# Which engine makes the low half of each expert weight: 24 on GpSimd, none on VectorE

## The chip, the cores and the metric

One core of a Trainium2 chip runs the whole program. The metric is the device time of one execution in microseconds (us), lower is better; a kernel's time is the median of its runs. In this text PE is TensorE, DVE is VectorE, ACT is ScalarE, POOL is GpSimd and SP is SyncE, which here only issues DMAs.

## The reference

Four batches of 1,024 tokens with 256 channels pass a cross attention to 64 context rows and then a mixture-of-experts feed-forward layer, each on a layer-normalised input and added to its residual.

```python
x = x + _L0_xattn_ref(_layernorm(x), ctx_768, Wq, bq, Wk, bk, Wv, bv, Wo, bo)   # 16 heads
# _L0_ffn_ref on the layer-normalised x, T = 4096 tokens, D = 256, H = 512, E = 8 experts, top 2
shared = _swiglu(xf, sh_gate, sh_up, sh_down)
w, idx = jax.lax.top_k(jax.nn.softmax(xf @ gate_w.T), 2)
comb = zeros((T, E)).at[arange(T)[:, None], idx].add(w / w.sum(-1))
g = silu(einsum('td,ehd->teh', xf, eg)); u = einsum('td,ehd->teh', xf, eu)
out = shared + einsum('ted,te->td', einsum('teh,edh->ted', g * u, ed), comb)
```

(The argument names are shortened.) All data are float32.

## The kernel before

TensorE multiplies in float16. To keep float32's accuracy each operand is held as two float16 numbers, a high half (the value rounded) and a low half (the value less its high half), and each product is the sum of three: high by high, high by low, low by high.

**The weights.** There are 27 weight matrices of 128 x 1024 numbers, numbered q: 0 to 2 are the shared expert's gate, up and down, and 3 to 26 are those of the 8 experts. Matrix q goes through four steps. SP loads it in float32 into slot q % 4 of a ring of four, `w_stage` (`load_w`, L449), and for q >= 4 first waits until q - 4 is split. ACT rounds it into its high half (`split_hi`, L705). Then one engine subtracts to make the low half: POOL (L629) where q is odd, DVE (`split_lo`, L960) where q is even. That subtraction counts up the semaphore `w_lo[q % 4]`, for which SP waits, and PE before it starts the experts (`weights_split`).

**Three stages.** Up to about 310 us runs the attention. Then comes the *shared stage*: 32 steps k, each a chunk of 128 hidden units of the shared expert on a group of 512 tokens (four steps make a group). Last comes the *expert stage*, 46 slots of gathered tokens.

**A step k of the shared stage.** PE does `up(k)` (24 matmuls of 512 columns, gate and up; the trace lists them in twelves) and then `down(k-1)` (12 matmuls of 256 columns). ACT runs SiLU (L764), in some steps a part of the second layer norm (`norm2`, L750 and L757), then `split_hi`, then the high half of the hidden activations (L778). DVE multiplies gate and up (L1150), at each group's first step adds the group before to `x_sb` (`add_shared`, L1190), in some steps does the layer norm's low half (`low_half`, L989, for which the transposes on SP's queue wait, L471) and reads the router's logits (L995); then comes `split_lo`, and last the low half of the hidden activations (L1183), for which `down(k)` on PE waits. Everything on an engine runs in program order.

**Which matrix in which step.** A table, `SPLITS`, gives the steps k = 2 to 13 the matrices q = k + 1 (3 to 14), and the steps k = 19 to 30 the matrices q = k - 4 (15 to 26). POOL follows by `w_hi`, the count of high halves. The routing runs on DVE in between: `best_two` at k = 11 (L1017 to L1036, ahead of matrix 12's split), `weights` and `places_in_expert` at k = 13 (L1041 to L1089, ahead of matrix 14's), and one-hot maps up to k = 18.

**POOL's queue** around the end of the shared stage: after matrix 21 (k = 25) it issues the stores of five finished groups of output (L622), a store of spare rows (L633) and the gathers for the first three expert slots (L603, four indirect DMAs); only then come its remaining splits, then the last three output stores, and the gathers and scatters of the expert stage.

The lines of `split_lo` and of POOL's loop:

```python
for q in range(1, 3 * (E + 1), 2):                      # POOL
    pool.wait_ge(w_hi, q + 1)
    pool.tensor_tensor(w[:, 1], w_stage[:, q % 4, :], w[:, 0], ALU.subtract).then_inc(w_lo[q % 4], 1)
    if q == 21:
        ...
if q % 2 == 0:                                          # DVE, split_lo(q)
    dve.wait_ge(w_hi, q + 1)
    dve.tensor_tensor(w[:, 1], w_stage[:, q % 4, :], w[:, 0], ALU.subtract).then_inc(w_lo[q % 4], 1)
```

Of the kernel before, what the change touches and what calls it, by code (L numbers as in the profile page):

```python
# [17 lines left out]
def build(nc, x, ctx_t, wq, bq, wk, bk, wv, bv, wo, bo, gate_t, w_all, out):  # L18
# [3 lines left out]
    E = w_all.shape[0] // 3 - 1  # L22
# [39 lines left out]
    with ExitStack() as ctx:  # L62
        def sb(name, shape, dt):
            return ctx.enter_context(nc.sbuf_tensor(name, shape, dt))
# [9 lines left out]
        w_sh = sb("w_sh", [P, 3, 2, 1024], F16)  # L74
        arena = sb("arena", [P, E * 3 * 2 * 1024], F16)
        w_rt = arena[:, :].rearrange("p (e m s n) -> p e m s n", e=E, m=3, s=2)
        w_qs = arena[:, :].rearrange("p (q s n) -> p q s n", q=3 * E, s=2)
# [429 lines left out]
        def _(pool):  # L507
# [90 lines left out]
            def gather(n):  # L598
                for r, i in zip(buffers(n), columns(n)):
                    if rank_of[n] >= 2:  # L600
                        pool.wait_ge(xt_got[r], 16 * uses(n))
                        pool.wait_ge(sp_w, same_kind(n, 2) + 1)
                    pool.indirect_dma_start(  # L603
                        out=gathered(r), out_offset=None, in_=rows_d,
                        in_offset=bass.IndirectOffsetOnAxis(ap=map_i[:, 0, i:i + 1], axis=0)).then_inc(x_got[r], 16)
# [14 lines left out]
            def store_out(g):  # L620
                pool.wait_ge(ffn_added, g + 1)
                pool.dma_start(out_tiles[:, g * GT:(g + 1) * GT, :],  # L622
                               x_sb[:, g * GT:(g + 1) * GT, :]).then_inc(out_stored, 16)

            AHEAD = 3
            for q in range(1, 3 * (E + 1), 2):
                w = w_sh[:, q] if q < 3 else w_qs[:, q - 3]
                pool.wait_ge(w_hi, q + 1)
                pool.tensor_tensor(w[:, 1], w_stage[:, q % 4, :], w[:, 0], ALU.subtract).then_inc(w_lo[q % 4], 1)  # L629
                if q == 21:  # L630
                    for g in range(NGB - 1):
                        store_out(g)
                    pool.dma_start(out[T:T + P, :], x_sb[:, 0, :]).then_inc(out_stored, 16)  # L633
                    pool.wait_ge(place_ready, 1)
                    pool.wait_ge(wt_stored, 16)
                    for r in range(XB):
                        pool.wait_ge(x2_stored[r], 16 * (NG // XB))
                    pool.wait_ge(gu_ready, FSX)
                    for n in range(AHEAD):
                        gather(n)  # L640
# [171 lines left out]
        def _(dve):  # L812
# [141 lines left out]

            def split_lo(q):

                if q % 2 == 0:
                    w = w_sh[:, q] if q < 3 else w_qs[:, q - 3]
                    dve.wait_ge(w_hi, q + 1)
                    dve.tensor_tensor(w[:, 1], w_stage[:, q % 4, :], w[:, 0], ALU.subtract).then_inc(w_lo[q % 4], 1)  # L960

            def unit(u):
                clip(u, 0)
                clip(u, 1)
                if known(u, 4):
                    residual(u - 4)
                    moments(u - 4)
                    mean_and_variance(u - 4)
                clip(u, 2)
                clip(u, 3)  # L970
                if known(u, 1):
                    normalise(u - 1)
                if u in (4, 6, 8):
                    split_lo(u // 2 - 2)
# [170 lines left out]
            def shared_step(k):  # L1145
# [32 lines left out]
                for w in splits_of(k):  # L1178
                    split_lo(w + 3)
# [421 lines left out]
```

## Time and profile before

| | |
|---|---|
| median of 3 runs | 825.28 us (819.78, 825.28, 825.73) |
| the profiled execution, its own time | 825.44 us |
| its span (first to last instruction) | 823.7 us |
| busy PE, DVE, ACT, POOL | 81%, 57%, 40%, 45% of the span |
| mean granted clock of TensorE | 0.882 of full speed |
| attention and start | 0 to about 319 us |
| shared stage, `down(0)` to `down(31)` | 328.82 to 513.5 us |
| expert stage | 513.35 us to the end |

An engine's busy share is an average over stages. A step's pace is read from PE's idle time ahead of a `down`, and from which instruction ended it. The chain of waits follows the work that ended last back from the end; a piece in it was what the rest waited for.

### The profile page before, as it was taken

The page shows a single profiled execution, that of the slowest core. Times are in us where ns is not written, and L with a number is a line of the kernel's source. Part 1 is how long each engine was busy: PE and PEld are TensorE (multiplying, and loading weights), DVE is VectorE, ACT ScalarE, POOL GpSimd, SP SyncE. Part 2 cuts the span into 40 slices and gives each one's busy share as a digit, 9 for nine tenths or more (in the row PEclk, how much of TensorE's full clock was granted, in tenths as well). Part 3 has the DMA queues.
Part 4 walks back from the last instruction along what each step waited for, and adds up shares of the span by engine and source line. Part 5 has one row for each costly group of instructions (what it writes and reads, how often), then busy time and mean ns, then how long its engine had stood idle before and what let it go on. Part 6 is the DMA issues. An engine that isn't in the chain of part 4 may idle for free.

```text
span 823.7 us, 16036 instructions
## 1 busy us (share of the span) xinstructions
PE 665.5 (81%) x5326; PEld 429.9 (52%) x5326; DVE 469.0 (57%) x1023; ACT 331.9 (40%) x548; POOL 373.9 (45%) x309
## 2 busy tenths in 40 slices
PE   3667676799888843878657898999999999999992
PEld 1223232244444531544334555777887878787881
DVE  1877777456566652565799766445444544445451
ACT  1044444466566716663401443333333333333330
POOL 3053536176667630122100244464667566666643
PEclk9986777656889976989869999999999999999996
DMA  7500000001111162577310256464665465555742
GB/s 200 180 1 0 1 0 0 1 14 27 33 33 34 34 116 51 154 164 207 119 29 1 76 163 204 105 103 77 100 111 100 82 101 99 97 93 97 105 65 33
DMA packets 108171, 66.12 MB, mean 80 GB/s; under 512 B 82947, under 2 KB 101317, under 8 KB 108101
## 3 DMA queue, kind: packets, MB, share of 16 engines
q1 hardware_dynamic: 93268, 41.91, 21.8%
q0 software_dynamic: 14832, 23.24, 16.1%
q8 instruction: 48, 0.79, 0.4%
q14 instruction: 23, 0.18, 0.1%
HBM read 29.47 MB, written 17.96 MB: 58 GB/s over the span
## 4 chain that ended last, share of the span: by engine, by line
PE 60%; DVE 18%; ACT 7%; issue 5%; DMA 3%; SPq 3%; POOL 2%; another core or an unknown queue 1%; POOLq 0%; ACTq 0%; DVEq 0%
PE bank L1248 57%; DVE bank L903 3%; DVE arena L853 3%; DVE hidden L1183 2%; SPq L471 2%; PE bank L1303 1%; ACT arena L680 1%; DVE arena L947 1%; DMA arena<-arena 1%; PE bank L1534 1%; POOL arena L592 1%; DVE x_sb L940 1%; ACT arena L687 1%; ACT arena L750 1%
## 5 line engine op out<-in xcount | busy, mean ns | idle before, releaser
L1248 PE MATMUL bank<-arena 128*128 128x34 f16 (+6 forms) x1284 | 145.0, 265 | 47.6 <-DVE bank L903 14.4
L1248 PE MATMUL bank<-qx,arena 128*128 128x256 f16 (+1 forms) x1584 | 157.8, 289 | 2.9 <-ACT arena L712 2.0
L616 POOL DMA_INDIRECT out<-w_stage,map_i x71 | 114.0, 1606 | 69.4 <-DMA out<-w_stage,map_i 23.7
L1248 PEld LDWEIGHTS bank<-arena 128*128 128x128 f16 (+2 forms) x1284 | 78.1, 111 | 118.7 <-DVE bank L903 35.4
L1248 PEld LDWEIGHTS bank<-qx,arena 128*128 (+1 forms) x1584 | 126.7, 102 | 25.6 <-ACT arena L712 4.7
L1217 DVE TENSOR_TENSOR hidden<-bank,hidden 128x512 f32<-128x512 f32 x71 | 49.1, 691 | 106.3 <-ACT hidden L793 75.3
L1248 PE MATMUL bank<-arena,w_stage 128*128 x852 | 104.7, 273 | 0.8 <-DVE w_stage L1236 0.4
L1248 PE MATMUL bank<-arena,qx 128*128 (+1 forms) x316 | 84.3, 391 | 25.6 <-DVE arena L853 15.6
L629 POOL TENSOR_TENSOR arena<-w_stage,arena 128x1024 f16<-128x1024 f32 x12 | 26.5, 2208 | 170.9 <-ACT arena L705 170.9
L592 POOL TENSOR_TENSOR arena<-arena 128x512 f16<-128x512 f32 x64 | 73.6, 1173 | 50.0 <-PE bank L1248 29.6
L603 POOL DMA_INDIRECT qx<-rows_d,map_i x71 | 71.7, 1010 | 52.9 <-DVE lane_w L1209 34.9
L1248 PE MATMUL bank<-qx,w_sh 128*128 128x512 f16 x384 | 94.2, 398 | 0.0
L793 ACT ACTIVATE hidden<-bank 128x512 f32<-128x512 f32 x71 | 42.4, 597 | 127.6 <-PE bank L1248 96.0
L1248 PEld LDWEIGHTS bank<-arena,w_stage 128*128 128x128 f16 x852 | 82.3, 98 | 17.4 <-issue 3.3
L1248 PE MATMUL bank<-w_sh,hidden 128*128 128x256 f16 x384 | 55.7, 303 | 26.4 <-DVE hidden L1183 26.4
L1236 DVE TENSOR_TENSOR w_stage<-hidden,w_stage 128x512 f16<-128x512 f32 x71 | 49.5, 697 | 43.1 <-ACT w_stage L805 36.4
L1248 PEld LDWEIGHTS bank<-arena,qx 128*128 128x128 f16 (+1 forms) x316 | 30.6, 98 | 70.8 <-issue 41.7
L903 DVE TENSOR_SCALAR bank<-bank 128x512 f32<-128x512 f32 x64 | 40.7, 688 | 43.9 <-PE bank L1248 43.9
L1248 PEld LDWEIGHTS bank<-qx,w_sh 128*128 128x128 f16 x384 | 39.5, 103 | 44.0 <-issue 8.3
L1248 PEld LDWEIGHTS bank<-w_sh,hidden 128*128 128x128 f16 x384 | 39.7, 108 | 41.3 <-DVE hidden L1183 32.2
L712 ACT ACTIVATE arena<-bank,arena 128x512 f32<-128x512 f32 x64 | 41.2, 687 | 47.1 <-PE bank L1248 46.8
L805 ACT CAST w_stage<-hidden 128x512 f16<-128x512 f32 x71 | 44.0, 619 | 39.7 <-DVE hidden L1217 33.6
(184 smaller groups left out, 757.3 us busy)
## 6 DMA issues: line engine op xcount, KB each, us to landing
w_stage<-in_w_all SPq DMA_DIRECT2D x27, 512.0 KB, 4.4
x_sb<-in_x SPq DMA_DIRECT2D x8, 512.0 KB, 4.6
rows_d<-arena SPq DMA_DIRECT2D x8, 512.0 KB, 3.7
out<-x_sb POOLq DMA_DIRECT2D x8, 512.0 KB
qx<-rows_d,map_i POOLq DMA_INDIRECT x71
qx<-qx SPq DMA_TRANSPOSE x71
out<-w_stage,map_i POOLq DMA_INDIRECT x71
arena<-arena SPq DMA_TRANSPOSE x32, 2.5
```

The costliest lines, as they stand in the source:

```text
L592: pool.tensor_tensor(p_l[:, u % 2, r], p_f[:, r], p_h[:, u % 2, r], ALU.subtract).then_inc(pl_ready, 1)
L603: pool.indirect_dma_start(out=gathered(r), out_offset=None, in_=rows_d, in_offset=bass.IndirectOffsetOnAxis(ap=map_i[:, 0, i:i + 1], axis= ...
L616: pool.indirect_dma_start(out=out, out_offset=bass.IndirectOffsetOnAxis(ap=map_i[:, 1, i:i + 1], axis=0), in_=y_sb[:, r], in_offset=None, ...
L629: pool.tensor_tensor(w[:, 1], w_stage[:, q % 4, :], w[:, 0], ALU.subtract).then_inc(w_lo[q % 4], 1)
L712: act.activation(p_f[:, r], bank[r][:, :], ACT.Exp, scale=exp_scale).then_inc(exp_ready, 1)
L793: act.activation(act_g[:, k % 2], bank[k % 2][:, :], ACT.Silu).then_inc(sp_silu, 1)
L805: act.copy(h_sp[:, k % 3, 0], h_f[:, k % 2]).then_inc(sp_hh, 1)
L853: dve.tensor_reduce(m_raw[:, s, i, bass.ts(hf, HH)], bank[4 + hf][:, :].rearrange("p (h k) -> p h k", h=HH), AX.X, ALU.max).then_inc(smax_ ...
L903: dve.tensor_scalar(bank[r][:, :], bank[r][:, :], CLIP, -CLIP, ALU.min, ALU.max).then_inc(st_clipped, 1)
L1217: dve.tensor_tensor(h_f[:, k % 2], bank[2 + k % 2][:, :], act_g[:, k % 2], ALU.mult).then_inc(sp_h, 1)
L1236: dve.tensor_tensor(h_sp[:, k % 3, 1], h_f[:, k % 2], h_sp[:, k % 3, 0], ALU.subtract).then_inc(sp_hl, 1)
L1248: return pe.matmul(o, a, b, start=first, stop=last, skip_group_check=not check)
```

## The change

The odd and even expert matrices are no longer shared out: POOL takes matrix 1 and then every matrix from 3 to 26, and DVE keeps only 0 and 2, both in the attention. Nothing else is edited.

```diff
-            for q in range(1, 3 * (E + 1), 2):
+            for q in (1, *range(3, 3 * (E + 1))):
                 w = w_sh[:, q] if q < 3 else w_qs[:, q - 3]
                 pool.wait_ge(w_hi, q + 1)
                 pool.tensor_tensor(w[:, 1], w_stage[:, q % 4, :], w[:, 0], ALU.subtract).then_inc(w_lo[q % 4], 1)
...
             def split_lo(q):
 
-                if q % 2 == 0:
-                    w = w_sh[:, q] if q < 3 else w_qs[:, q - 3]
+                if q in (0, 2):
+                    w = w_sh[:, q]
                     dve.wait_ge(w_hi, q + 1)
```

POOL's instructions from the end of the attention to the first expert slots, as a difference (`arena` holds the expert weights, `w_stage` the loaded float32, `x_sb` the output):

```order
 L585 TENSOR_TENSOR arena<-arena 128x2x256 x2
 L629 TENSOR_TENSOR w_sh<-w_stage,w_sh 128x1024
-L629 TENSOR_TENSOR arena<-w_stage,arena 128x1024 x10
+L629 TENSOR_TENSOR arena<-w_stage,arena 128x1024 x19
 L622 DMA out<-x_sb 128x4x256 x5
 L633 DMA out<-x_sb 128x256
 L603 DMA qx<-rows_d,map_i 128x264 x4
-L629 TENSOR_TENSOR arena<-w_stage,arena 128x1024 x2
+L629 TENSOR_TENSOR arena<-w_stage,arena 128x1024 x5
 L622 DMA out<-x_sb 128x4x256 x3
 L603 DMA qx<-rows_d,map_i 128x264 x5
```

Ahead of the stores and gathers stand 19 expert splits instead of 10, behind them five (matrices 22 to 26) instead of two (23 and 25).

DVE's instructions at step k = 11, the end of `best_two` and what follows it:

```order
 L1034 TENSOR_TENSOR arena<-arena 128x32x8
 L1036 TENSOR_TENSOR w<-m 128x32
-L960 TENSOR_TENSOR arena<-w_stage,arena 128x1024
 L1183 TENSOR_TENSOR hidden<-hidden 128x512
 L1150 TENSOR_TENSOR hidden<-bank,hidden 128x512
```

The split of matrix 12 is gone from between the routing and the step's low half; the same row is gone at k = 13 (matrix 14) and at ten other steps, 12 rows in all. PE, ACT and SP have the same instructions in the same order as before.

## Rows read from the trace of the kernel before

**Rows 1.** The page, busy time, share and instructions of each engine.

```profile
PE 665.5 (81%) x5326; PEld 429.9 (52%) x5326; DVE 469.0 (57%) x1023; ACT 331.9 (40%) x548; POOL 373.9 (45%) x309
```

**Rows 2.** By stretch: length, busy PE, PEld, DVE, ACT, POOL (instructions), clock, DMA share, GB/s.

```profile
380.00:454.00 74.00, 48.36 (x282) 28.08 (x279) 58.15 (x100) 16.55 (x24) 4.49 (x2) 0.82 0.26 77
454.00:512.00 58.00, 53.06 (x325) 31.14 (x325) 39.24 (x48) 26.54 (x39) 22.81 (x18) 1.00 0.51 157
512.00:602.00 90.00, 89.07 (x747) 70.46 (x748) 42.26 (x91) 31.49 (x49) 49.81 (x41) 1.00 0.52 95
```

**Rows 3.** The chain of waits, pieces at DVE's splits: start, length, what.

```profile
398.06 1.06 DVE arena L960
...
417.51 1.00 issue
...
465.63 1.14 DVE arena L960
...
498.80 1.76 DVE arena L960
```

**Rows 4.** By line: duration in ns, least, median and most, first and last start.

```profile
L960 DVE TENSOR_TENSOR arena<-w_stage,arena x12: 1206/1226/1765, 343.5 to 506.9; 128x1024 f16<-128x1024 f32 x12
...
L629 POOL TENSOR_TENSOR arena<-w_stage,arena x12: 2126/2127/2831, 336.2 to 501.8; 128x1024 f16<-128x1024 f32 x12
...
L1183 DVE TENSOR_TENSOR hidden<-hidden x32: 673/686/2618, 328.1 to 511.2; 128x512 f16<-128x512 f32 x32
```

**Rows 5.** The timeline, downs 17 to 20: start, length, instruction, [idle before, by whom].

```profile
454.38 1.49 PE L1248 MATMUL bank<-w_sh,hidden 128*128 128x256 f16 x12 [1.84 <-DVE hidden L1183]
...
458.29 1.47 PE L1248 MATMUL bank<-w_sh,hidden 128*128 128x256 f16 x12
...
458.98 1.04 ACT L705 CAST arena<-w_stage 128x1024 f16<-128x1024 f32 x1
...
460.10 2.13 POOL L629 TENSOR_TENSOR arena<-w_stage,arena 128x1024 f16<-128x1024 f32 x1 [58.41 <-ACT arena L705]
460.57 2.20 DVE L1183 TENSOR_TENSOR hidden<-hidden 128x512 f16<-128x512 f32 x1 [0.76 <-ACT hidden L778]
...
462.83 1.48 PE L1248 MATMUL bank<-w_sh,hidden 128*128 128x256 f16 x12 [0.48 <-DVE hidden L1183]
...
467.43 1.49 PE L1248 MATMUL bank<-w_sh,hidden 128*128 128x256 f16 x12 [0.53 <-DVE hidden L1183]
```

**Rows 6.** The timeline in the attention: two POOL instructions in a row, one of DVE.

```profile
231.37 3.25 POOL L592 TENSOR_TENSOR arena<-arena 128x512 f16<-128x512 f32 x2
232.28 1.32 DVE L960 TENSOR_TENSOR w_sh<-w_stage,w_sh 128x1024 f16<-128x1024 f32 x1 [2.11 <-ACT w_sh L705]
```

**Rows 7.** The timeline, steps 11 and 13: ACT's rounding, DVE's routing.

```profile
390.35 1.04 ACT L705 CAST arena<-w_stage 128x1024 f16<-128x1024 f32 x1
...
392.18 0.42 DVE L1019 TENSOR_TENSOR arena<-logits,m 128x256 f32<-128x256 f32 x1
...
406.56 1.04 ACT L705 CAST arena<-w_stage 128x1024 f16<-128x1024 f32 x1
...
407.90 0.19 DVE L1043 TENSOR_TENSOR w<-w 128x32 f32<-128x32 f32 x1
```

**Rows 8.** The timeline, the end of the shared stage, steps 25 to 29.

```profile
487.56 4.03 POOL L622 DMA_DIRECT2D out<-x_sb  x5
...
497.32 2.15 POOL L629 TENSOR_TENSOR arena<-w_stage,arena 128x1024 f16<-128x1024 f32 x1
...
497.60 1.28 DVE L1190 TENSOR_TENSOR x_sb<-x_sb,bank 128x512 f32<-128x512 f32 x2
...
501.23 1.49 PE L1248 MATMUL bank<-w_sh,hidden 128*128 128x256 f16 x12 [1.07 <-DVE hidden L1183]
...
505.14 1.47 PE L1248 MATMUL bank<-w_sh,hidden 128*128 128x256 f16 x12
```

**Rows 9.** By line, SP's 27 weight loads: issue to landing.

```profile
DMA to landing us min/median/max: 3.4/4.4/9.0
```

## The prediction

> **What bounds the kernel now.** I read the busy shares first [rows 1]: PE 81%, DVE 57%, POOL 45%. They say only that DVE has more to do than POOL, so I read the stages next [rows 2]. In the expert stage PE is busy 89.07 of 90 us, and the change leaves that stage's instructions alone; it can only start it earlier or later. The question is when the last `down` of the shared stage ends. From 380 to 454 us DVE is busy 58.15 of 74 us and PE 48.36: the routing on DVE sets the pace. From 454 to 512 us PE is busy 53.06 of 58, at full clock, so 5 us are open there. The chain of waits names DVE's splits at five places [rows 3]: 1.06 us at 398, 1.00 at 417 (shown as "issue": the split of matrix 14 starts at 417.37 and the low half behind it at 418.51), 1.14 at 465.6, as much again at 482.6 (1.13), and 1.76 at 498.8. That is 6.1 us in all, the most that dropping these instructions can take off this path. The other seven splits on DVE stand beside waits that end later.
>
> **What is removed, what is added.** DVE loses 12 subtractions of 1.23 us, about 15 us of busy time; POOL gains 12 of 2.13 us, 25.6 us [rows 4]. POOL has the room. What matters is where the new ones lie, and what they do to DVE.
>
> **The lock.** Look at step 19, whose matrix (15) is POOL's already [rows 5]. ACT's rounding ends at 460.02, POOL subtracts from 460.10 to 462.23, and DVE's low half L1183, which starts at 460.57, takes 2.20 us where its median is 0.69 [rows 4]. It ends at 462.77, 0.54 after POOL: it stood still while POOL ran. Both read two operands from SBUF. `add_shared` (L1190), with one operand in PSUM, runs 1.28 us beside a POOL subtraction that started at 497.32 and is not slowed [rows 8]. So a split on POOL is not free for DVE: POOL starts it the moment ACT is done, and L1183 of the same step comes 0.5 us later and waits for its end. With the split on DVE, L1183 ends 0.08 + 1.14 + 0.68 = 1.9 us after the rounding; with POOL, 2.75 us after. A moved split makes L1183 about 0.85 us later where the rounding is what came last, and earlier only where DVE's own queue was late.
>
> The Trainium skill, "SBUF — State Buffer", section "Who interferes with whom", has this rule: VectorE's second SBUF port is GpSimd's only one, whoever issues first keeps it for the whole instruction, and an instruction with two SBUF inputs needs it. "Perfetto Trace Analysis", section "Optimizing Scalar/DVE Operations", therefore warns that moving work between those two "might not help". By the rule the gain is not 6.1 us but what is left after the waits below; this trace agrees with it (2.20 us for 0.69).
>
> **Steps 2 to 10.** The five odd matrices (3, 5, 7, 9, 11) behave as before. Of the moved ones, matrix 4 makes `down(3)` about 0.9 us later, but `down(4)` waits for a chain over ACT and SP's transposes that the split does not touch; the SP queue then runs 0.9 us late for one group and has that slack. Matrix 6 queues behind matrix 5 on POOL, 8 and 10 end before PE needs them. I put this stretch at 0; with the cover gone it would be 0.9 us for each of the four.
>
> **Step 11, `best_two`.** The rounding of matrix 12 ends at 391.39 [rows 7], so POOL subtracts from 391.46 to 393.59. DVE's first two-operand routing instruction, L1019, starts at 392.18 and takes 0.42: it would end at about 393.9 instead of 392.6, and the chain behind it is 1.3 us late. In return the split at its end is gone, 399.03 - 397.79 = 1.24. Sum +0.05, plus 0.05 as PE's counting matmuls now wait for the routing and not beside the split: **+0.1**.
>
> **Step 13.** Rounding ends at 407.60, POOL runs 407.7 to 409.8 (0.1 more by the shift). L1043 at 407.90 waits [rows 7]: 409.95 against 408.09, +1.87. Gone from the chain is 418.51 - 417.37 = 1.14. Sum **+0.73**. So at 454 us the kernel is 0.8 us late: a split at the end of a serial routing chain costs DVE 1.2, the same split on POOL at its start costs it up to 2.1.
>
> **Steps 19 to 25.** PE alone repeats a step in 3.91 us (454.38 to 458.29). A step with a POOL split needs 8.45 us from the `down` two steps before (454.38 to 462.83) [rows 5]. Written out without the 0.8 us shift, `down(20)` comes at max(462.83 + 3.9, 458.29 + 8.45) = 466.74 instead of 467.43, 0.7 us earlier. But `down(21)` is 462.83 + 8.45 = 471.28 against 471.34 before: it hangs on `down(19)`, not on 20. Now every step has a POOL split, so two steps take 8.45 us instead of 7.8, and what the steps with `add_shared` gain is lost again in the next. `down(25)` is 0.1 us earlier; that is all.
>
> **Steps 26 to 31.** POOL's stores and gathers stand between, from 487.56 until its next split at 497.32 [rows 8]. Steps 26 and 27 therefore meet no split, and both are at PE's pace as before: `down(27)` at 495.95. From 497.2 matrices 22, 23 and 24 lie ready for POOL in a row. L1183 of step 28 is ready at 498.7, waits for matrix 22 to end at 499.35 and is done at 499.9: `down(28)` at 500.0 against 501.23, where DVE's split had collided and taken 1.76 [rows 3]. POOL goes on at 499.9 with 23, at 502.0 with 24 until 504.15; L1183 of step 29, ready at 502.2, is done at 504.7, and `down(29)` comes at 504.8 against 505.14 [rows 8]. `down(31)` follows `down(29)` by 6.85 us as before. So this stretch gives **-0.3**; it gives -1.1 if L1183 of step 29 gets ahead of matrix 24, which it misses by 0.2 us.
>
> **The queues it moves past.** Matrix 22 is now split at 499.4, not 491.3, and SP's load of matrix 26 waits for it, in front of the first transposes of the expert stage (502.5). A load lands 3.4 to 9.0 us after its issue, 4.4 in the median [rows 9], so at about 503.9; ACT wants it at 504.6. Cost 0, with 0.7 us to spare. The output stores of groups 5 and 6 leave POOL at about 509.7 instead of 503.9 and still precede the third (515). The last split ends at 509.7, ahead of PE's need at 513. Cost 0.
>
> **Sum.** 0.1 + 0.73 - 0.3 = +0.5 us on the profiled execution's 825.44 (span 823.7 and 1.7 around it): 826.0. The profiled execution is 0.2 above the median of the runs shown, which I neglect. The bounds of the terms: steps 2 to 10 from 0 to 3.6 (four times 0.9) and no gain, as none of their splits is in the chain; steps 11 and 13 from -2.1 (POOL's turn finds a gap) to +2.1 (nothing comes back from the dropped split at 11); the end from -1.1 to +0.3. Together 822 to 831, and 1% of the time, what a measurement of this kernel can tell from none, is 8.3 us.
>
> **The rivals.** (a) *The lock costs less than it seems*, since POOL's subtraction slips beside small routing instructions and L1183 does not hold PE. Then the chain's 6.1 us come off: 825.4 - 6.1 = 819.3; with half of it 822.4. For it speaks the 6.1 us of chain, against it the 2.20 us in [rows 5]. Even this stays within 1%.
>
> (b) *POOL does not let DVE in between two of its instructions.* In steps 27 to 30 four splits then run from 497.2 to 505.8 without a gap, L1183 of step 28 is done at 506.3, `down(29)` at 510.2 and `down(31)` at 517.1, 5.1 us late; at step 4 another 2.1 us (matrix 6 right behind 5); with the 0.8 of the routing 8.0: 833.4. It decides wherever two splits lie ready at once. Against it: at 232.28 DVE waited with a second POOL instruction ready behind the first; DVE ran first, until 233.60, and the POOL pair took 3.25 us, longer than two of 1.16 [rows 6].
>
> (c) *The load of matrix 26 comes late.* At the longest landing, 9.0 us [rows 9], it lands at 508.4; ACT rounds until 509.5, POOL splits until 511.7, L1183 of step 30 is done at 512.3, then step 31's L1150, ACT and L1183 follow (0.6 + 0.7 + 0.7), and `down(31)` comes at 514.3 instead of 511.7: 2.6 us, 828.6. It decides from a landing of over 6 us. For it: stores of 2.6 MB go out from 487 on; against it: the load is issued when they are nearly through.
>
> (d) *It does nothing that shows*: covered by the forecast.
>
> **How the numbers follow.** Forecast (with d) 0.72, (a) 0.12, (b) 0.06, (c) 0.07, anything else 0.03. The runs shown spread from 819.78 to 825.73, so the median itself can lie some 5 us low with nothing changed; the range therefore begins at 820, where (a) begins too, and ends at 830.5, above (c). (b) is left out. Over 1% faster would take more than the chain has at DVE's splits: 0.03. Over 1% slower takes (b) and a little more, or (b) with (c): 0.05. Within 1%: 0.92.
>
> **What would show it.** L1183 with over 2 us in nearly all of the steps 3 to 10 and 19 to 25, not in every second; L1019 at 1.7 us and L1043 at 2.1; `down` rows in 19 to 25 at 8.45 us for two; POOL's five splits behind the gathers spaced 2.1 to 2.7 us; a DVE busy time that falls by much less than 15 us. The forecast is wrong if the routing (391 to 454 us) ends earlier than before, if L1183 of step 28 waits for more than one split, or if ACT waits for a load at step 30.

## The result and the profile after

| | before | after |
|---|---|---|
| median | 819.78 us (15 runs, 815.88 to 825.73) | 830.71 us (15 runs, 825.78 to 835.8) |
| the profiled execution, its own time | 825.44 us | 831.19 us |
| its span | 823.7 us | 829.3 us |
| busy PE, DVE, ACT, POOL | 81, 57, 40, 45% | 80, 57, 40, 48% |
| mean granted clock | 0.882 | 0.884 |
| `down(0)` starts | 328.82 us | 327.27 us |
| `down(27)` starts | 496.09 us | 492.35 us |
| first expert matmul | 513.35 us | 517.20 us |

The changed kernel is slower: ratio 1.0121, with 95% between 1.0088 and 1.0154, which is 9.9 us (7.2 to 12.6) of 819.78. The two profiled executions differ by 5.6 us in span. The profiled one of before lay 5.7 us above its median (825.44 against 819.78), that of after only 0.5, so two spans show less than the medians do. For this reason I compare places inside the program and not the spans: the time from one `down` to another.

The busy shares, and the two lines that the change touches, on the page of after (a line's columns: busy us, mean ns of one, idle before it and who ended it):

```profile
PE 664.8 (80%) x5326; PEld 428.8 (52%) x5326; DVE 471.5 (57%) x1011; ACT 331.8 (40%) x548; POOL 398.9 (48%) x321
...
L629 POOL TENSOR_TENSOR arena<-w_stage,arena 128x1024 f16<-128x1024 f32 x24 | 52.0, 2174 | 157.4 <-ACT arena L705 157.4
...
L1183 DVE TENSOR_TENSOR hidden<-hidden 128x512 f16<-128x512 f32 x32 | 49.3, 1541 | 22.6 <-ACT hidden L778 22.6
```

DVE has 12 instructions less than in [rows 1] and is busy 2.5 us longer, 471.5 for 469.0. L1183 took 35.8 us in all before and takes 49.3 now: DVE no longer makes these low halves, but it waits inside its next instruction with two SBUF operands (at the routing steps that is L1019 and L1043).

Where the time went, in us between the starts of two instructions of PE:

| from, to | before | after |
|---|---|---|
| `down(10)` to `down(11)` (`best_two`) | 10.12 | 10.24 |
| `down(12)` to `down(13)` (weights and places) | 13.38 | 13.99 |
| `down(18)` to `down(27)` | 37.80 | 37.68 |
| `down(27)` to `down(28)` | 5.14 | 10.24 |
| `down(28)` to the first expert matmul | 12.12 | 14.61 |

The last two rows are the tail of the shared stage, 17.26 us before and 24.85 after: 7.6 of the 9.9 us. The chain of waits of after in this tail (start, length, what) has one piece that answers to the split in [rows 3]:

```profile
495.06 7.48 DVE hidden L1183
502.54 0.05 issue
502.59 9.85 PE bank L1248 x48
```

The timeline there (start, length, instruction, count of instructions in the row, idle before):

```profile
492.35 1.47 PE L1248 MATMUL bank<-w_sh,hidden 128*128 128x256 f16 x12
...
492.64 0.95 POOL L603 DMA_INDIRECT qx<-rows_d,map_i  x1 [0.30 <-issue]
...
493.61 8.37 POOL L629 TENSOR_TENSOR arena<-w_stage,arena 128x1024 f16<-128x1024 f32 x4
...
495.06 7.47 DVE L1183 TENSOR_TENSOR hidden<-hidden 128x512 f16<-128x512 f32 x1
...
502.59 2.74 PE L1248 MATMUL bank<-w_sh,hidden 128*128 128x256 f16 x12 [6.17 <-DVE hidden L1183]
...
505.12 3.40 PE L1248 MATMUL bank<-qx,w_sh 128*128 128x512 f16 x12
...
509.06 1.04 ACT L705 CAST arena<-w_stage 128x1024 f16<-128x1024 f32 x1
...
510.17 2.13 POOL L629 TENSOR_TENSOR arena<-w_stage,arena 128x1024 f16<-128x1024 f32 x1 [8.19 <-ACT arena L705]
510.64 2.20 DVE L1183 TENSOR_TENSOR hidden<-hidden 128x512 f16<-128x512 f32 x1 [0.76 <-ACT hidden L778]
```

POOL issues its last gather at 492.64 and begins at 493.61 with the splits of matrices 22 to 25, four in a row, which end at 501.98. L1183 of step 28 comes up at 495.06, in the first of them, and ends at 502.53, 0.55 us after the last. PE stands 6.17 us. What follows is slower too: `down(28)` takes 2.74 us and the twelve matmuls behind it 3.40, where 1.47 and 2.75 are their times elsewhere. TensorE was granted 2.4 GHz until it stood; the granted clock fell during the pause, and `down(28)` ran at the 1.2 GHz level:

```profile
451.00:496.40 45.40, 43.56 (x264) 24.92 (x261) 28.92 (x35) 21.10 (x31) 26.11 (x19) 1.00 0.46 152
502.59:505.33 2.74, 2.74 (x13) 1.94 (x14) 1.23 (x2) 0.62 (x1) 0.00 (x0) 0.50 0.01 1
```

(Columns as in [rows 2]; the granted clock is third from the end, 1.00 up to the pause and 0.50 for `down(28)`.) That costs 1.27 us on `down(28)` and 0.65 on the twelve behind it, and so `down(29)` follows `down(28)` by 5.77 us where it was 3.91 in [rows 8], 1.86 more. At step 30 the split of matrix 26, the row at 510.17, holds L1183 again, and `down(30)` is 0.6 late. `down(31)` makes that up, but PE then pauses 0.50 us ahead of the first expert matmul, which it did not before, so the first expert matmul is the 0.6 us late again; why, I did not settle.

### The profile page after: what moved, and what is told of

Its sections match the earlier page's. It is cut to its first block, busy times and chain, and to the rows that moved or that the text cites. A ratio compares the mean times of both kernels' runs of the same rounds, so it can differ in the third digit from the quotient of the medians.

```text
span 829.3 us, 16035 instructions
## 1 busy us (share of the span) xinstructions
PE 664.8 (80%) x5326; PEld 428.8 (52%) x5326; DVE 471.5 (57%) x1011; ACT 331.8 (40%) x548; POOL 398.9 (48%) x321
## 4 chain that ended last, share of the span: by engine, by line
PE 58%; DVE 19%; ACT 7%; issue 5%; SPq 4%; DMA 3%; POOL 2%; another core or an unknown queue 1%; POOLq 0%; ACTq 0%; DVEq 0%
PE bank L1248 55%; DVE hidden L1183 3%; DVE bank L903 3%; DVE arena L853 3%; SPq L471 2%; PE bank L1303 1%; ACT arena L680 1%; DVE arena L947 1%; POOL arena L592 1%; PE bank L1534 1%; DVE x_sb L940 1%; DMA arena<-arena 1%; ACT arena L705 1%; ACT arena L687 1%; ACT arena L750 1%
## 5 line engine op out<-in xcount | busy, mean ns | idle before, releaser
L629 POOL TENSOR_TENSOR arena<-w_stage,arena 128x1024 f16<-128x1024 f32 x24 | 52.0, 2174 | 157.4 <-ACT arena L705 157.4
L1183 DVE TENSOR_TENSOR hidden<-hidden 128x512 f16<-128x512 f32 x32 | 49.3, 1541 | 22.6 <-ACT hidden L778 22.6
```

The costliest lines, as they stand in the source:

```text
L1183: dve.tensor_tensor(h_l[:, hc % 2], h_f[:, hc % 2], h_h[:, hc % 2], ALU.subtract).then_inc(hl_ready, 1)
```

## The experiments

The theory after this view is that the loss is the tail, and that its cause is POOL: once in a row of ready splits, it lets DVE in only at the end. There are two rivals. The loss could come from the moved splits in general, through the routing and the steps. Or DVE would normally be let in, and something particular in this row of four keeps it out.

In the changed kernel the choice is one loop on POOL and one condition on DVE; most of the experiments edit these alone. Times come with the ratio to before, run on the same chip; its median was 819.98 us for the first four, 822.6 for `only_22`, `all_dve` and `pick`, and 823.31 for `idle_first`. The ratio need not be exactly that of the two medians.

**tail_dve.** Matrices 22, 24 and 26 back on DVE, the other nine moved.

```diff
-for q in (1, *range(3, 3 * (E + 1))):
+ON_VECTOR = (0, 2, 22, 24, 26)
+for q in [q for q in range(1, 3 * (E + 1)) if q not in ON_VECTOR]:
```

> Matrices 22, 24 and 26 go back to VectorE, the other nine moved ones stay on GpSimd, so no two splits lie ready behind the gathers except 23 and 25. Theory S (GpSimd keeps the shared port over a run of ready splits, and L1183 of step 28 starves): the 7 us lost after down(27) come back, L1183 of step 28 takes under 3 us, the time is 1 to 2 us above before (routing steps 11 and 13), ratio 1.00. Theory L (each of the twelve moved splits costs its own 0.5 to 1 us of lock): nine twelfths of the loss stay, ratio 1.009.

823.74 us, ratio 1.0035 (1.0006 to 1.0064), which is 2.9 us (0.5 to 5.2), and the tail took 17.27 us, as before.

```profile
493.60 2.15 POOL L630 TENSOR_TENSOR arena<-w_stage,arena 128x1024 f16<-128x1024 f32 x1
...
495.04 1.79 DVE L961 TENSOR_TENSOR arena<-w_stage,arena 128x1024 f16<-128x1024 f32 x1
```

DVE comes up at the same place, but POOL's row is one split long. Without the three, the tail's loss is gone.

**tail_only.** The reverse: only 22, 24 and 26 moved.

```diff
+ON_VECTOR = (0, 2, 4, 6, 8, 10, 12, 14, 16, 18, 20)
```

> Only matrices 22, 24 and 26 move to GpSimd; 4 to 20 stay on VectorE. Theory S: L1183 of step 28 stands still for 6 to 8 us as in the changed kernel, and nearly the whole loss is there: 7 to 9 us, ratio 1.009 to 1.011. Theory L: three twelfths of the loss, 2.5 us, ratio 1.003.

829.32 us, ratio 1.0105 (1.0062 to 1.0147), 8.6 us. The tail took 24.83 us, and the two routing intervals were those of before (10.12 and 13.38).

```profile
492.77 8.37 POOL L630 TENSOR_TENSOR arena<-w_stage,arena 128x1024 f16<-128x1024 f32 x4
...
494.28 7.42 DVE L1184 TENSOR_TENSOR hidden<-hidden 128x512 f16<-128x512 f32 x1
```

Three moved splits of twelve carry nearly the whole loss.

**first_only.** Only 4 to 14 moved, those of the steps 3 to 13.

```diff
+ON_VECTOR = (0, 2, 16, 18, 20, 22, 24, 26)
```

> Only matrices 4 to 14 move; 16 to 26 stay on VectorE. My steps 2 to 13: +0.1 at step 11 and +0.7 at step 13, no more, ratio 1.001. Theory L: six twelfths, 5 us, ratio 1.006. If the routing chain costs each split's whole 2.13 us, +2.5 us, 1.003.

821.11 us, ratio 1.002 (0.9992 to 1.0048). The routing intervals were 10.25 and 14.00 and the tail 17.21: a cost of 0.7 us, too small for the ratio to confirm.

**paced.** The changed kernel, but from matrix 22 on POOL waits until L1183 of the step after the matrix's own is done, so that no two splits lie in a row.

```diff
 for q in (1, *range(3, 3 * (E + 1))):
     pool.wait_ge(w_hi, q + 1)
+    if q >= 22:
+        pool.wait_ge(hl_ready, q + 6)
```

> All twelve are on GpSimd as in the changed kernel, but ahead of each split from 22 on GpSimd also waits until the low half of step q + 5 is done (L1183 of steps 27 to 31), so no two splits follow each other and VectorE is let in. Theory S: L1183 of steps 28 to 31 takes 0.7 us each, the 5 us stall at down(28) is gone, and what is left is the last split, done 2.1 us after the last L1183: before plus 1 to 3 us, ratio 1.002 to 1.004. If the loss came from the late load of matrix 26 or the late output stores instead, it stays or grows: ratio 1.012 or more.

823.66 us, ratio 1.0039 (1.0009 to 1.0068), and the tail took 18.17 us.

```profile
499.11 2.15 POOL L632 TENSOR_TENSOR arena<-w_stage,arena 128x1024 f16<-128x1024 f32 x1
...
500.56 1.26 DVE L1186 TENSOR_TENSOR hidden<-hidden 128x512 f16<-128x512 f32 x1
...
512.73 2.13 POOL L632 TENSOR_TENSOR arena<-w_stage,arena 128x1024 f16<-128x1024 f32 x1 [1.70 <-DVE hidden L1186]
...
516.02 2.76 PE L1251 MATMUL bank<-arena,qx 128*128 x12 [1.89 <-issue]
```

`down(28)` came 4.03 us after `down(27)`, better than before's 5.14. But the last split waits in turn until 512.73 and ends at 514.86, and PE, whose program waits for all the splits before the experts, stands 1.89 us (the trace names no releaser for this pause). The order "one split, then DVE" removes the stall; my wait most likely put the smaller one at the end.

**only_22.** Only matrix 22 moved; POOL then has 22 and 23 behind the gathers.

```diff
+ON_VECTOR = (0, 2, 4, 6, 8, 10, 12, 14, 16, 18, 20, 24, 26)
```

> Of the twelve only matrix 22 moves: behind the gathers GpSimd finds 22 and 23 ready, a run of two and not of four; VectorE has its own split of matrix 24 and then L1183 in step 28. If a run of ready splits keeps the port to its end: VectorE's split of 24 stands still until about 4.2 us after GpSimd's first one began and takes 3.8 to 4 us (1.8 in the kernel before), and down(28) comes about 7.3 us after down(27) (5.14 before). If VectorE is let in after the first: its split takes 1.8 us as before, and L1183 behind it may be the one that waits.

A single run, 827.89 us, so no ratio; the tail took 23.66.

```profile
492.74 4.22 POOL L631 TENSOR_TENSOR arena<-w_stage,arena 128x1024 f16<-128x1024 f32 x2
...
494.21 3.84 DVE L964 TENSOR_TENSOR arena<-w_stage,arena 128x1024 f16<-128x1024 f32 x1
...
497.21 2.83 POOL L631 TENSOR_TENSOR arena<-w_stage,arena 128x1024 f16<-128x1024 f32 x1 [0.24 <-ACT arena L709]
...
497.98 2.60 DVE L1187 TENSOR_TENSOR hidden<-hidden 128x512 f16<-128x512 f32 x1
```

Two in a row are enough: DVE's split comes up at 494.21, in the first, and ends after the second. It is late by one more subtraction; then L1187, which is L1183 here, collides with matrix 25 as well, which the expected 7.3 us had left out. `down(28)` is 9.14 us behind `down(27)`.

**probe.** But in [rows 6] DVE was let in, and so it was in after at step 4, where POOL had two splits ready (the last row's 2.20 is one turn of POOL, not two):

```profile
346.90 4.66 POOL L629 TENSOR_TENSOR arena<-w_stage,arena 128x1024 f16<-128x1024 f32 x2 [4.45 <-ACT arena L705]
...
347.38 2.20 DVE L1183 TENSOR_TENSOR hidden<-hidden 128x512 f16<-128x512 f32 x1 [0.24 <-ACT hidden L778]
```

So I measured the turn-taking by itself, in a small kernel with the same two instructions on a copy of the input, in trials that differ in how and when they start.

```python
pool.wait_ge(start, starts)                             # one trial on POOL
for i, w in enumerate(widths):
    ...                                                 # in some trials a wait ahead of the later ones
    pool.tensor_tensor(p_lo[:, i, 0:w], x_f[:, 0:w], hi[:, 0:w], ALU.subtract).then_inc(p_done, 1)
...
dve.wait_ge(go, n + 1)                                  # and on DVE
dve.tensor_tensor(h_l[:, :], h_f[:, :], h_h[:, :], ALU.subtract).then_inc(d_done, 1)
```

> No part of the model is computed: the kernel copies x and runs ten trials in which GpSimd does two or four subtractions in a row (f32 less f16 from SBUF) and VectorE one subtraction of 512 columns that becomes ready at a chosen moment. Trials 1, 2: four of 1024 columns, no wait between, VectorE ready about 0.4 and 1.4 us after the first began. 3, 4: the same with a wait between that is long satisfied. 5 to 7 and 10: two, the second's wait satisfied about 2, 0.7, 0.3 and 0.3 us after the first began, VectorE ready before (5, 6) or after it (7, 10). 8, 9: four of 512 columns. If order of readiness decides: VectorE runs after the first GpSimd instruction in 5 and 6 and after the whole run in all others. If VectorE always starves behind ready ones whatever the order: also in 6. If the moment within the instruction decides (early ones get in, late ones not): in after the first in 1, 3, 5, 6, 9, 10, and not in 2, 4, 7.

In all ten trials DVE was let in after the subtraction that it met, whether the later ones lay ready or not (1.15 to 2.44 us on DVE).

```profile
17.36 8.80 POOL L72 TENSOR_TENSOR p_lo<-x_sb,hi 128x1024 f16<-128x1024 f32 x4 [16.92 <-ACT scratch L90]
17.60 2.43 DVE L105 TENSOR_TENSOR h_l<-h_f,h_h 128x512 f16<-128x512 f32 x1 [17.60 <-ACT scratch L90]
...
26.81 8.80 POOL L72 TENSOR_TENSOR p_lo<-x_sb,hi 128x1024 f16<-128x1024 f32 x4 [0.65 <-ACT scratch L90]
27.93 1.55 DVE L105 TENSOR_TENSOR h_l<-h_f,h_h 128x512 f16<-128x512 f32 x1 [7.90 <-ACT scratch L90]
```

"A row of POOL's shuts DVE out" is thus false as a rule. Something of the kernel's tail was missing.

**probe2.** Fifteen trials: DVE arriving later in the first subtraction (1 to 3), DVE coming straight from additions with a PSUM operand, as in the tail (4 to 6), and four gathers issued by POOL directly ahead of the row (7 to 15, in 13 to 15 two stores as well).

```diff
 pool.wait_ge(start, n + 1)
+for i in range(stores):
+    pool.dma_start(dump[:, i, :], ...).then_inc(sw, 16)
+for i in range(gathers):
+    pool.indirect_dma_start(out=got[:, i], ...).then_inc(sw, 16)
```

> No part of the model is computed: fifteen trials, in each GpSimd does four subtractions of 1024 columns in a row and VectorE one of 512 columns with two SBUF operands. They differ in what the first probe did not have. Trials 1 to 3: VectorE ready late in GpSimd's first instruction (about 1.3 to 1.8 us after it began). 4, 5, 6: one or two additions with a PSUM operand run on VectorE directly before its subtraction, so that it comes up with no idle time, as L1183 behind add_shared does. 7 to 9: four gathers stand on GpSimd's queue directly before the four subtractions. 10 to 12: gathers and additions. 13 to 15: two stores of 2 MB besides. Late arrival: VectorE starves (6 to 7 us) in 2, 3 and 5 to 15 where it comes late, not in 4. Coming up directly behind another VectorE instruction: it starves in 4, 5, 6, 10 to 14, not in 1 to 3 and 7 to 9. Gathers ahead of the run: it starves in 7 to 15 alone. None of the three: it takes 0.7 to 2.6 us everywhere.

Trials 1 to 6 took 0.82 to 1.84 us on DVE, trials 7 to 15 took 7.67 to 9.39. One of the first kind (trial 5) and two of the second (9 and 7):

```profile
54.94 8.80 POOL L92 TENSOR_TENSOR p_lo<-x_sb,hi 128x1024 f16<-128x1024 f32 x4 [0.57 <-ACT scratch L112]
...
56.40 1.21 DVE L132 TENSOR_TENSOR h_l<-h_f,h_h 128x512 f16<-128x512 f32 x1
...
108.37 0.95 POOL L86 DMA_INDIRECT got<-in_x,idx  x1 [0.30 <-issue]
109.34 8.34 POOL L92 TENSOR_TENSOR p_lo<-x_sb,hi 128x1024 f16<-128x1024 f32 x4
110.28 7.95 DVE L132 TENSOR_TENSOR h_l<-h_f,h_h 128x512 f16<-128x512 f32 x1 [7.21 <-ACT scratch L112]
...
78.35 0.95 POOL L86 DMA_INDIRECT got<-in_x,idx  x1 [0.30 <-issue]
78.83 9.39 DVE L132 TENSOR_TENSOR h_l<-h_f,h_h 128x512 f16<-128x512 f32 x1 [11.85 <-ACT scratch L112]
79.32 8.34 POOL L92 TENSOR_TENSOR p_lo<-x_sb,hi 128x1024 f16<-128x1024 f32 x4
```

The gathers make the difference. POOL's four take 8.34 us when it keeps DVE out and 8.80 when it lets it in once. Trial 7 says more: DVE came up at 78.83, while POOL was still issuing its last gather and 0.49 us before the first subtraction, and it was shut out all the same, until 88.22. So being there first did not help DVE. Yet an issue alone holds nothing up: in after, L1183 ran in its usual 0.69 us at 486.21, while POOL issued stores (485.67 to 487.91), and at 490.73, while it issued a gather (490.10 to 491.08). Waits on a semaphore long counted up, between the subtractions of trials 11 to 15, did not let DVE in either.

**probe3.** Is it the gather, any DMA that POOL issues, the traffic, or a state that stays? Five subtractions of POOL, DVE released by the first and so there in the second; ahead of them nothing, one or four gathers, four plain stores, and between the DMAs and the row nothing, a memset, or a wait until they have landed.

```diff
+if between == "memset":
+    pool.memset(mark[:, :], 0.0).then_inc(marked, 1)
+if between == "landed":
+    pool.wait_ge(sw, moved)
```

> No part of the model is computed: ten trials, in each GpSimd does five subtractions in a row and VectorE one, which waits for the first of the five and so comes up in the second. Ahead of the five stand: 1 nothing, 2 four plain stores, 3 one gather, 4 four gathers, 5 nothing, 6 four gathers and a small memset, 7 four gathers and a wait until they have landed, 8 nothing, 9 four gathers (subtractions of 512 columns), 10 four plain stores and a wait until they have landed. If gathers directly ahead of the run are what shuts VectorE out: it takes about 2.4 us in 1, 2, 5, 8 and 10, and until the end of the run (8 us) in 3, 4 and 9. If any DMA that GpSimd issues does it: also in 2. If it is a state that stays once a gather has run: also in 5 and 8. 6 and 7 show what ends it: I expect the wait of 7 to, and the memset of 6 not to.

| ahead of POOL's row | DVE's instruction |
|---|---|
| nothing (three trials, two of them after trials with gathers) | 2.51, 2.52, 2.52 us |
| four plain stores | 8.73 us |
| one gather | 8.74 us |
| four gathers | 8.74 us |
| four gathers and a memset | 8.74 us |
| four gathers, then a wait until they landed | 2.52 us |
| four stores, then a wait until they landed | 2.52 us |
| four gathers, subtractions of 512 columns | 4.87 us |

```profile
31.16 10.41 POOL L88 TENSOR_TENSOR p_lo<-x_sb,hi 128x1024 f16<-128x1024 f32 x5
33.40 8.73 DVE L109 TENSOR_TENSOR h_l<-h_f,h_h 128x512 f16<-128x512 f32 x1 [11.34 <-POOL p_lo L88]
...
104.08 0.95 POOL L79 DMA_INDIRECT got<-in_x,idx  x1 [0.30 <-issue]
106.78 10.88 POOL L88 TENSOR_TENSOR p_lo<-x_sb,hi 128x1024 f16<-128x1024 f32 x5 [1.76 <-DMA got<-in_x,idx]
109.01 2.52 DVE L109 TENSOR_TENSOR h_l<-h_f,h_h 128x512 f16<-128x512 f32 x1 [9.58 <-POOL p_lo L88]
```

A row that follows POOL's own DMA issue without a wait shut DVE out until its end, with gathers and with plain stores; a wait that POOL really had to wait in ended this. It is not the traffic: with one gather, with four, and with four and a memset, the last gather, issued at 43.11, 59.81 and 87.44, had landed 2.8 us later, before DVE's subtraction came up at 46.38, 63.01 and 90.69, and it was shut out all the same. Whether it is the wait itself or the time that POOL stands idle was not told apart, and what in the engine does it stays open.

**idle_first.** The same in the kernel: only at matrix 22, POOL waits for the high half of matrix 24 instead of its own, which comes after the last gather has been issued. All five splits then still lie in one row.

```diff
-pool.wait_ge(w_hi, q + 1)
+pool.wait_ge(w_hi, 25 if q == 22 else q + 1)
```

> The changed kernel with one number altered: ahead of the split of matrix 22, behind the gathers, GpSimd waits for the high half of matrix 24 (about 0.5 us later than it is free) and not of 22. All five splits still follow each other with nothing between. If it is the step from a DMA issue straight into a run that shuts VectorE out, this half microsecond of waiting lets it in: L1183 of step 28 takes 1.5 to 2.5 us and not 7.5, down(28) comes 4 to 4.6 us after down(27) and not 10.2, ratio to before 1.002 to 1.005. If a run of ready splits alone does it, nothing changes: 10.2 us, ratio 1.012.

824.36 us, ratio 1.0007 (0.9982 to 1.0033), and the tail took 16.92 us, with `down(28)` 4.55 us behind `down(27)`.

```profile
498.60 0.95 POOL L603 DMA_INDIRECT qx<-rows_d,map_i  x1 [0.30 <-issue]
...
500.13 11.82 POOL L629 TENSOR_TENSOR arena<-w_stage,arena 128x1024 f16<-128x1024 f32 x5 [0.57 <-issue]
...
501.03 1.77 DVE L1183 TENSOR_TENSOR hidden<-hidden 128x512 f16<-128x512 f32 x1
...
504.50 0.85 DVE L1183 TENSOR_TENSOR hidden<-hidden 128x512 f16<-128x512 f32 x1 [0.76 <-ACT hidden L778]
```

With 0.57 us between the last gather and the row, POOL subtracts five times without a pause and DVE gets in three times. One moved wait takes the whole tail loss away. It also shows what the twelve moves do to DVE without the lock-out: DVE is busy 465.4 us here, 3.6 less than before, though 12 subtractions of 1.23 us are gone.

**all_dve.** If DVE pays for POOL's splits by waiting, the opposite change should gain: every expert matrix on DVE, only matrix 1 on POOL (whose stores and gathers keep their place behind step 25 by a wait for matrix 21's high half).

```diff
+ON_VECTOR = (0, 2, 3, 4, ..., 25, 26)
```

> The other direction: every expert matrix on VectorE, GpSimd keeps only matrix 1, its stores and gathers stay where they were. If a GpSimd split costs the step more than a VectorE split (L1183 2.75 us after the rounding against 1.9), steps 19 to 27 go at 3.9 us, the steps with add_shared at 4.6: 36.5 us from down(18) to down(27) against 37.8, step 28 at 4.6 against 5.1, and some 1 us in steps 2 to 6: 2 to 3 us faster, ratio 0.997. If VectorE's load were what holds this stage: 5 us slower or more.

816.89 us, ratio 0.9931 (0.99 to 0.9962): 5.7 us faster than before. Its page:

```profile
PE 653.6 (80%) x5326; PEld 425.2 (52%) x5326; DVE 466.2 (57%) x1035; ACT 331.9 (41%) x548; POOL 349.4 (43%) x297
```

DVE has 12 instructions more than before and is busy 2.8 us less (466.2 for 469.0): all 32 of its L1187, which is L1183 here, take 0.68 to 0.69 us, 21.9 us in all for 35.8. From `down(18)` to `down(27)` the kernel needs 36.50 us for 37.80, as expected, and in the tail 16.71 for 17.26. These two places give 1.8 of the 5.7 us, and I had expected 2 to 3 in all; where the rest comes from is not shown. A step, split and low half:

```profile
488.13 1.22 DVE L964 TENSOR_TENSOR arena<-w_stage,arena 128x1024 f16<-128x1024 f32 x1
...
489.26 0.68 DVE L1187 TENSOR_TENSOR hidden<-hidden 128x512 f16<-128x512 f32 x1
```

**pick.** All on DVE except 13, 16, 20 and 24: the steps with `add_shared`, where DVE has most to do.

```diff
+ON_VECTOR = (0, 2, 3, ..., 12, 14, 15, 17, 18, 19, 21, 22, 23, 25, 26)
```

> GpSimd takes only the matrices whose steps have add_shared on VectorE (13, 16, 20, 24), where its subtraction runs beside an instruction with an operand in PSUM; VectorE takes all others. Expected by the lock as measured: every step from 19 to 27 at PE's pace of 3.9 us, 35.2 us against 37.8, step 28 0.5 us earlier, 1 us in steps 2 to 6, nothing lost in the routing: 3 to 5 us faster than before, ratio 0.994 to 0.997. If balance of busy time were what counts, slower than before.

819.15 us, ratio 0.9941 (0.9913 to 0.997): not to be told from `all_dve`. From `down(18)` to `down(27)` it took 36.41 us, not the expected 35.2: the `add_shared` steps did not come down to PE's 3.9 us but took 4.53.

```profile
478.29 2.13 POOL L631 TENSOR_TENSOR arena<-w_stage,arena 128x1024 f16<-128x1024 f32 x1 [14.12 <-ACT arena L709]
...
479.20 1.77 DVE L1187 TENSOR_TENSOR hidden<-hidden 128x512 f16<-128x512 f32 x1
```

DVE comes free at 479.2, waits for POOL until 480.4 and is done at 480.97. With the split its own it would be 479.2 + 1.14 + 0.68 = 481.0: a tie, even in the steps where DVE has most to do.

## Why the prediction was wrong, and what of it held

It said 826.0, in 820.0 to 830.5 and within 1%. The measured median lies 0.2 us above the range, and the change against before is 1.2% (0.9 to 1.5), so probably not within 1%. The forecast of the change was +0.5 us and the measured one is 9.9. That the absolute numbers look closer comes from the base: 825.44, which I took as the median, was 5.7 us above what fifteen runs gave.

- **Step 11, +0.1:** measured +0.12; L1019 took 1.69 us, as foreseen. **Step 13, +0.73:** +0.61; L1043 took 1.95.
- **Steps 19 to 25, -0.1:** -0.12 from `down(18)` to `down(27)`, with L1183 at 2.20 in most steps. That what one step gains the next gives back was right. (The forecast's sum had left this -0.1 out.)
- **Steps 2 to 10, 0:** not to be tested. `down(1)` to `down(10)` took 54.84 us before and 53.20 after, but between 51.29 and 57.93 over the profiled executions of the ten versions, a spread larger than any effect I forecast there.
- **Steps 26 to 31, -0.3: the step that failed**, by 7.9 us. The sentence is "L1183 of step 28 is ready at 498.7, waits for matrix 22 to end at 499.35 and is done at 499.9". It rests on POOL letting DVE in between two ready splits, and POOL did not: L1183 waited for four, 5.1 us more to `down(28)`. The other 2.5 us I did not have in the sum at all: TensorE at its lower level after the stall (1.86), and 0.6 from matrix 26's split on. `idle_first` shows what the sentence assumed: 16.92 us for 17.26, the -0.3 of the forecast, once POOL has waited.
- **Rival (b)** had the mechanism and, for the tail, the price of 5.1 us. Its other place, step 4, did not occur; the row at 346.90 is why. I gave it 0.06 because [rows 6] spoke against it. That row was true but of another case: POOL had come to it from a wait, as the row that starts its sequence in the trace of before shows (below), and in the tail it comes from a gather. Of (b)'s 8.0 us the 2.1 at step 4 did not come; the clock (1.86) and the 0.6 from matrix 26's split, which (b) did not have, came in their place.

```profile
228.02 2.27 POOL L592 TENSOR_TENSOR arena<-arena 128x512 f16<-128x512 f32 x2 [1.60 <-PE bank L1248]
```

- **Rival (c)** did not occur: ACT rounded matrix 26 at 509.06, 0.5 us behind the start of its SiLU as in every step. **Rival (a)** fails by the waits that did come: of the twelve moved steps, L1183 took 7.47 us in 28, 2.2 in 3, 7, 22 and 30 and 1.1 to 1.7 in 9, 20 and 24, and L1019 and L1043 waited in 11 and 13. But the sign that I named for my forecast, over 2 us in nearly all of the steps 3 to 10 and 19 to 25, did not come in full: it was 10 of 15 steps, where before had 7.
- **What remains.** 7.6 (tail), 0.7 (routing) and -0.1 give 8.2 of 9.9 us, inside the interval. I did not find a place for the other 1.7. The expert stage took 310.3 us before and 312.1 after, but over the ten versions, whose matmuls there are the same, it took 309.4 to 312.8, longest in `all_dve`, the fastest of them; so the difference can't be counted as an effect of the change.

The Trainium skill, "SBUF — State Buffer", section "Who interferes with whom", says that GpSimd has only the port pair that is VectorE's second one, and that whoever issues first gets it for the whole instruction. The trace agrees where POOL comes from a wait (2.52 us for 0.68). Behind POOL's DMAs it differs (8.74): there POOL kept DVE out for a whole row of instructions, even where DVE had come first (9.39).

## What to carry to other kernels

Moving an elementwise instruction with two SBUF operands from VectorE to GpSimd may take little off VectorE: here 12 moves of 1.23 us left it 2.5 us busier, and only 3.6 us less busy in `idle_first`, without the lock-out. Giving VectorE the 12 that GpSimd had before made the kernel 0.7% faster than before. Before trusting that VectorE gets in after one GpSimd instruction, look at what GpSimd did directly ahead: behind its own DMA issues, put a wait that has to be waited for, or keep its SBUF work out of there. And a row that speaks against a rival counts only if it comes from the rival's own situation; [rows 6] did not.

## What the runs showed of the hardware that I had not expected

- Behind a DMA issued by GpSimd itself (a gather or a plain store, one or four), a row of GpSimd's subtractions let VectorE in only at its end: 8.73 and 8.74 us for five, 7.5 in the kernel for four. With a wait between (0.57 us in the kernel, 1.76 and 2.98 in `probe3`), or with no DMA ahead, it got in after the subtraction it met: 2.51 and 2.52 us for five. A memset in between changed nothing (8.74).
- VectorE was shut out even when it came up first, 0.49 us before the row and during the issue of the last gather: 9.39 us. An issue with no subtraction behind it did not hold it up (0.69 us). Its additions with an operand in PSUM, in the same place, took 0.68 and 0.69 us and were not held.
- A stall of 6.17 us of TensorE, entered at the granted 2.4 GHz, was followed by 12 matmuls at the 1.2 GHz level, in 2.74 us instead of 1.47. In `only_22` a stall of 5.08 us was too (2.74).
